# Reordered semaphore waits, a new table of places and 18 spare matmuls per chunk in a one-core AdaLN, Mamba and mixture-of-experts block

## What is computed

```
mod = silu(c) @ wmod                        # six rows of 256 per sequence: sa ca ga sb cb gb
h = layernorm(x) * (1 + ca) + sa
x = x + ga * mamba(h)                       # rmsnorm, in_proj, causal conv of 4 taps, silu,
                                            # x_proj -> dt, B, C; delta = softplus(dt_proj(dt))
                                            # scan over the sequence: s = s*exp(delta*A) + delta*B*u
                                            # y = sum_s(s*C) + u*D; out_proj(y * silu(z)) + h
h = layernorm(x) * (1 + cb) + sb
x = x + gb * (shared(h) + routed(h))        # 16 experts, top 4 by a sigmoid gate
```

## Time and profile before

| | before |
|---|---|
| median of 3 runs | 2980.88 us (2977.16 to 2983.09) |
| profiled execution, its time | 2980.19 us |
| profiled execution, its span | 2978.4 us |
| PE / DVE / ACT / POOL busy | 2431.5 / 2277.2 / 2129.4 / 2397.0 us |
| mean granted TensorE clock | 0.922 of 2.4 GHz |
| HBM read and written | 166.29 MB, 17.87 MB |

### The profile page before, as it was taken

The page is one execution under the profiler, slowest core; times in us unless marked ns, Lnnn a source line. Parts: engine busy times, 40 slices in busy tenths (PEclk is TensorE's granted clock), DMA queues, the critical chain, the costliest instruction groups (busy, mean ns, idle before and its releaser), DMA issues.

```text
span 2978.4 us, 52216 instructions
## 1 busy us (share of the span) xinstructions
PE 2431.5 (82%) x16084; PEld 1908.7 (64%) x16084; DVE 2277.2 (76%) x3495; ACT 2129.4 (71%) x4033; POOL 2397.0 (80%) x2382
## 2 busy tenths in 40 slices
PE   3557988888797888979888797888979788897879
PEld 1335767667576665757667575766757666676767
DVE  4777778787787878778787877878777787877753
ACT  4786877778686777868677787767868777785641
POOL 1887898889788888888888888888978878897842
PEclk7657999999899999999999899999989999998999
DMA  1775777867676785767677677776757777676841
GB/s 67 195 172 127 167 159 164 179 135 161 147 170 157 165 177 132 163 158 162 155 156 178 138 163 158 156 171 150 167 135 169 160 165 172 135 159 140 179 102 57
DMA packets 154563, 455.99 MB, mean 153 GB/s; under 512 B 22280, under 2 KB 24968, under 8 KB 154032
## 3 DMA queue, kind: packets, MB, share of 16 engines
q0 software_dynamic: 73728, 268.47, 48.2%
q1 hardware_dynamic: 80560, 184.20, 19.9%
HBM read 166.29 MB, written 17.87 MB: 62 GB/s over the span
## 4 chain that ended last, share of the span: by engine, by line
POOL 21%; issue 20%; PE 18%; DVE 15%; ACT 14%; DMA 6%; DVEq 1%; POOLq 0%; ACTq 0%; SPq 0%
POOL db_sb L669 10%; PE bank_ps L1413 8%; DVE states L1150 5%; PE moe_ps L1431 4%; POOL y_sb L681 3%; POOL act L712 3%; DMA y_sb<-c_rows 3%; DMA th_p<-x_dram 3%; ACT c_rows L886 3%; ACT da_ps L913 3%; PE rows_ps L1349 2%; DVE bank_ps L1097 2%; POOL y_sb L690 2%; DVE act L1231 2%; DVE act L1237 1%
## 5 line engine op out<-in xcount | busy, mean ns | idle before, releaser
L669 POOL TENSOR_TENSOR db_sb<-du_sb,b_sb 128x512 f32<-128x512 f32 x1024 | 1575.2, 1710 | 80.3 <-DVE states L1150 79.8
L886 ACT ACTIVATE c_rows<-rows_ps,xd_sb 128x512 f32<-128x512 f32 x1024 | 684.8, 684 | 186.4 <-PE rows_ps L1349 93.9
L1349 PE MATMUL rows_ps<-ident,states 128*128 128x128 f32 x4096 | 646.8, 291 | 177.6 <-ACT c_rows L886 104.9
L913 ACT ACTIVATE da_ps<-delta,a_sb 128x512 f32<-128x512 f32 x1024 | 704.4, 692 | 93.2 <-DVE states L1150 91.5
L712 POOL TENSOR_TENSOR act<-act,w_sb 128x256 f32<-128x256 f32 x512 | 580.8, 1185 | 224.7 <-DMA w_sb<-w_dram 119.4
L681 POOL DMA_DIRECT2D y_sb<-c_rows x512 | 608.2, 1195 | 149.9 <-DMA y_sb<-c_rows 77.1
L1431 PE MATMUL moe_ps<-eout_sb,act 128*128 128x256 f32 x2304 | 621.5, 395 | 103.8 <-POOL act L712 101.6
L1150 DVE TENSOR_TENSOR_SCAN states<-da_ps,carry,db_sb 128x512 f32<-128x512 f32 x512 | 649.3, 1276 | 54.1 <-ACT da_ps L913 52.3
L1349 PEld LDWEIGHTS rows_ps<-ident,states 128*128 128x128 f32 x4096 | 512.6, 150 | 273.8 <-DVE states L1150 123.6
L1413 PE MATMUL bank_ps<-h2T_high,ein_w_high 128*128 128x256 f16 x2304 | 643.2, 279 | 36.0 <-DVE h2T_low L1133 15.0
L1150 DVE TENSOR_TENSOR_SCAN states<-da_ps,db_sb 128x512 f32<-128x512 f32 x512 | 617.4, 1215 | 69.2 <-ACT da_ps L913 68.3
(11 more groups left out here) (169 smaller groups left out, 2633.8 us busy)
## 6 DMA issues: line engine op xcount, KB each, us to landing
y_sb<-c_rows POOLq DMA_DIRECT2D x512, 512.0 KB, 5.5
b_sb<-b_dram SPq DMA_DIRECT2D x128, 512.0 KB, 5.1
w_sb<-w_dram SPq DMA_DIRECT2D x256, 256.0 KB, 4.4
th_p<-x_dram SPq DMA_DIRECT2D x16, 512.0 KB, 8.2
r_dram<-conv SPq DMA_DIRECT2D x16, 512.0 KB, 2.8
x<-r_dram SPq DMA_DIRECT2D x16, 512.0 KB, 5.8
out_dram<-x SPq DMA_DIRECT2D x32, 256.0 KB, 2.3
mod_p<-mod_dram SPq DMA_DIRECT2D x7, 384.0 KB, 11.2
```

The lines of the kernel that those rows point to most:

```text
L669: pool.tensor_tensor(db_sb[:, n % NDB, :], du_sb[:, slots[t][0][0], b, :], b_sb[:, k % NBPAIR, s % BPAIR, :], ALU.mult).then_inc(sem["scal ...
L886: ac.activation(c_rows[:, n % NCR, j % CPAIR, :], rows_ps[j % 2][:, :], ACT.Copy, scale=xd_sb[:, slots[t][0][0], j, s:s + 1]).then_inc(sem ...
L913: ac.activation(da_ps[n % NDA][:, :], delta[:, slots[t][0][0], b, :], ACT.Exp, scale=a_sb[:, b, s:s + 1]).then_inc(sem["exp_done"], 1)
L1349: last = pe.transpose(rows_ps[j % 2][:, b * P:b * P + P], states[:, step % 2 * NB + b, j * P:j * P + P], ident[:, :])
```

## The change

There are four parts, with no change in what is computed.

1. In seven steps the waits are written in another order or cut down: `scaled` has `scan_done` first, `e_weigh` has the bank's semaphore first, `x_norm` has `x_rstd_done` first, `dtp` has the read of `xd` first, `rows` has `c_scales` first for j above 0, `tap` waits for `xi_centered` and then `halo_set` at k = 0 and for the tap before it alone at k above 0, and `dt_low` waits for both copies of `dt_high`.
2. The table of places is new throughout: `SHIFT`, `PLACE`, `FIRST`, `LAST`, `START` and the scalars. `PLACE` now has an entry for nearly every step.
3. `keep_awake` puts 10 matmuls of 128x256 f16 ahead of `y_t` of j = 0, and 8 ahead of `h2_t` of k = 0, into the bank that this step is about to fill.
4. `r_load` and `z_tanh` of the first mixed chunk wait for `ein_low_done`.

```diff
-SLOT = 70.6876
+SLOT = 70.5981
-SHIFT = {"b_load": -2.314, ... "c_add": 0.79, ... "w_t": 1.126, ... "y_gate": -0.101, ...}
+SHIFT = {"a_made": 2.299, ... "c_add": 1.155, ... "w_t": 1.841, ... "y_gate": -0.262, ...}
...
                     def scaled(t, s, b):
+                        if n >= NDB:
+                            pool.wait_ge(sem["scan_done"], n - NDB + 1)
                         pool.wait_ge(sem[f"b_in{k % NBPAIR}"], 16 * (k // NBPAIR + 1))
...
-                        pool.wait_ge(sem["scan_done"], max(0, n - NDB + 1))
...
                     def e_weigh(t, u):
+                        pool.wait_ge(*bank_read(("expert_in", t, u)))
                         pool.wait_ge(sem[f"w_in{k % NWROWS}"], 16 * (k // NWROWS + 1))
-                        pool.wait_ge(*bank_read(("expert_in", t, u)))
...
                     def x_norm(t, half):
+                        ac.wait_ge(sem["x_rstd_done"], nP(t) + 1)
                         ac.wait_ge(*bank_room(key))
-                        ac.wait_ge(sem["x_rstd_done"], nP(t) + 1)
...
                     def tap(t, b, k):
-                        v.wait_ge(sem["halo_set"], n + 1)
-                        v.wait_ge(sem["xi_centered"], n + 1)
-                        v.wait_ge(sem["tapped"], (CONV - 1) * n + k)
+                        if k:
+                            v.wait_ge(sem["tapped"], (CONV - 1) * n + k)
+                        else:
+                            v.wait_ge(sem["xi_centered"], n + 1)
+                            v.wait_ge(sem["halo_set"], n + 1)
...
                     def rows(t, s, j):
-                        pe.wait_ge(sem["scan_done"], (step + 1) * NB)
-
                         before = (step, j - 2) if j >= 2 else (step - 1, j + 2)
+                        if j == 0:
+                            pe.wait_ge(sem["scan_done"], (step + 1) * NB)
                         if before[0] >= 0:
                             pe.wait_ge(*c_scales(*before))
+                        if j > 0:
+                            pe.wait_ge(sem["scan_done"], (step + 1) * NB)
...
                     def y_t(t, j):
+                        if j == 0:
+                            keep_awake(("y_t", t, 0), 10)
...
+                    def keep_awake(key, n):
+
+                        pe.wait_ge(*bank_room(key))
+                        for _ in range(n):
+                            pe.matmul(bank(key)[:, 0:2 * P], in_w16[0][:, 0, 0:P], in_w16[0][:, 0, 0:2 * P], start=True, stop=True)
...
                     def h2_t(t, k):
+                        if k == 0:
+                            keep_awake(("h2_t", t, 0), 8)
```

More of the change, by code:

```diff
@@ L160 @@
-PLACE = {"b_load_0": 0.173, "b_load_3": -0.295, "b_load_4": 0.013, "b_load_7": 1.807, "c_scale_2": 0.046, "carry_0": -0.001,
[52 rows of a table removed]
-FIRST = {"b_store": 0.125, "dt_bias": 0.034, "dt_high": -0.092, "dtp": 0.026, "ein_low": -4.541, "h_rms": 0.889, "h_scale": 0.293,
-         "hn_high": -0.177, "hn_low": -1.03, "in_low": -1.842, "r_add": -0.475, "soft_ln": -0.603, "tap": 0.219, "u_tanh": 1.112,
-         "x_load": 0.132, "x_rstd": 5.921, "x_scale": -0.544, "xi": 2.127, "xi_copy": 0.024}
-LAST = {"e_mul": -0.008, "e_weigh": -0.199, "expert_in": -0.512, "expert_out": -0.749, "h2_high": 0.25, "h2_low": 0.658, "h2_t": 0.387,
-        "op_gate": -0.447, "out_add": 0.012, "r_load": -3.075, "w_load": 0.015, "w_store": -2.166, "w_t": -0.691, "x1_norm": -0.005,
-        "x1_rstd": -1.397, "x1_stat": 0.167, "y_evac": 0.514, "z": -0.362}
@@ L219 @@
-START = {"constants": 0.018, "ct_tanh": -1.588, "first_loads": 5.582, "fold": 1.987, "in_high": -3.563, "in_low": 0.718, "mod0": 0.251,
-         "mod_rows": -0.032, "mod_store": -0.045, "mods": 1.704, "out_scale": -2.535}
+LEAD_P0, LEAD_P, LEAD_M = 16.5692, 7.9826, 18.1414
+TICK, ROUTED, UNITS_END = 1.4598, 16.0092, 63.8809
+SOFT = 45.3931
+Z_AHEAD, Y_SOON, Y_LATE = 0.8485, -5.3218, 0.8267
+SLOT = 70.5981
+SHIFT = {"a_made": 2.299, "b_load": -0.655, "b_store": -0.03, "c_add": 1.155, "c_scale": 0.694, "carry": 0.739, "constants": 6.369,
+         "ct_silu": 7.993, "ct_tanh": 5.83, "delta": -0.292, "dt_bias": -0.13, "dt_high": -0.389, "dt_low": -0.659, "dtp": -0.013,
+         "du": 0.224, "e_act": -0.2, "e_mul": -0.161, "e_tanh": -0.423, "e_weigh": 0.864, "ein_high": 5.595, "ein_load": 4.207,
+         "ein_low": 1.18, "eout_fold": -4.167, "eout_load": 10.16, "exp": 1.021, "expert_in": -0.233, "expert_out": 0.79,
+         "first_loads": 0.924, "fold": 2.039, "gather": 0.59, "h2_high": 0.858, "h2_low": 1.341, "h2_scale": 0.171, "h2_t": 1.098,
+         "h_rms": -0.968, "h_scale": -0.068, "h_square": -0.404, "hn_high": -0.18, "hn_low": 0.343, "hn_t": -0.781, "in_high": -2.432,
+         "in_low": -2.541, "logit": -0.221, "logit_exp": 2.022, "mod0": 0.093, "mod0_gate": 9.566, "mod0_rows": 8.026,
+         "mod_m_load": -2.113, "mod_p_load": -4.442, "mod_rows": 8.536, "mod_store": -10.248, "mods": 6.814, "norm_lift": -8.849,
+         "op": 1.435, "op_gate": 1.25, "out_add": 0.237, "out_gate": 0.005, "out_scale": -12.936, "out_store": 1.491, "r_add": 3.969,
+         "r_gate": 0.223, "r_load": 1.079, "r_store": -6.015, "router": 1.458, "rows": 0.368, "scaled": 0.661, "scan": -0.15,
+         "skip": 0.192, "skip_evac": 0.341, "skip_t": 0.166, "soft_exp": -1.198, "soft_ln": 0.767, "tap": 0.086, "u": -0.826,
+         "u_tanh": 0.017, "w_evac": 0.533, "w_load": -0.824, "w_store": -2.476, "w_t": 1.841, "x1": 1.398, "x1_norm": -0.282,
+         "x1_rstd": -1.462, "x1_stat": 1.215, "x_load": -1.249, "x_norm": 0.894, "x_rstd": 0.076, "x_scale": 0.261, "x_shift": 0.165,
+         "x_stat": 0.314, "xd": -0.63, "xd_evac": -0.536, "xd_t": 0.416, "xd_t_evac": -0.528, "xi": 0.233, "xi_center": 0.049,
+         "xi_copy": 0.007, "y_evac": 0.755, "y_gate": -0.262, "y_t": 0.841, "z": -0.858, "z_gate": -0.839, "z_tanh": -0.616}
@@ new lines @@
+PLACE = {"b_load_0": 0.352, "b_load_1": 3.063, "b_load_2": 7.901, "b_load_3": -5.114, "b_load_4": 0.869, "b_load_5": 3.166,
[49 rows of a table added]
+         "in_low": 0.416, "logit": 0.537, "logit_exp": 0.204, "mod_m_load": -1.192, "mod_p_load": 0.549, "op_0": 0.553, "op_1": 0.135,
+         "op_2": 0.151, "op_3": -5.521, "op_gate_0": -0.207, "op_gate_1": -0.256, "op_gate_2": 0.574, "op_gate_3": -9.207,
+         "out_add_0": -0.142, "out_add_1": -0.151, "out_gate_0": 0.018, "out_gate_1": -0.445, "out_store_0": 1.142, "out_store_1": 2.785,
+         "r_add": -0.421, "r_gate": 0.252, "r_load": 0.166, "r_store": 4.589, "router": -0.089, "rows_0": -0.061, "rows_1": -0.193,
[21 rows of a table added]
@@ new lines @@
+FIRST = {"b_store": -1.691, "delta": -7.942, "dt_bias": -5.55, "dt_high": 0.322, "dt_low": 0.284, "dtp": -0.316, "du": 15.142,
+         "ein_high": 2.29, "ein_load": 1.427, "ein_low": -2.424, "h_rms": -7.043, "h_scale": -2.667, "h_square": 0.779, "hn_high": -2.392,
+         "hn_low": -2.331, "hn_t": -1.045, "in_high": 9.103, "in_low": -7.464, "r_add": -2.869, "r_gate": -3.859, "r_store": 9.187,
+         "skip": 0.46, "skip_evac": 7.151, "skip_t": 2.867, "soft_exp": 3.454, "soft_ln": 1.178, "tap": 0.991, "u": 2.33, "u_tanh": 0.596,
+         "x_load": -1.459, "x_norm": 0.639, "x_rstd": -0.049, "x_scale": 0.35, "x_shift": 0.09, "x_stat": 2.908, "xd": -5.521,
+         "xd_evac": -1.259, "xd_t": 0.226, "xd_t_evac": -0.902, "xi": -4.74, "xi_center": 1.94, "xi_copy": -0.671}
@@ new lines @@
+LAST = {"e_act": -0.086, "e_mul": 0.001, "e_tanh": 0.024, "e_weigh": 5.36, "expert_in": 0.948, "expert_out": 1.413, "h2_high": 1.147,
+        "h2_low": -2.551, "h2_scale": -1.666, "h2_t": -3.41, "logit": 1.396, "logit_exp": 0.191, "op": -0.871, "op_gate": 0.209,
+        "out_add": 1.16, "out_gate": 0.978, "out_store": -0.147, "r_load": 1.398, "router": 0.022, "w_evac": -1.369, "w_load": 2.655,
+        "w_store": 2.436, "w_t": 0.633, "x1": 0.207, "x1_norm": -3.031, "x1_rstd": -2.619, "x1_stat": 0.228, "y_evac": 0.006,
+        "y_gate": -0.421, "y_t": -0.772, "z": -3.279, "z_gate": -0.688, "z_tanh": -0.619}
@@ L223, in place @@
+START = {"a_made": 0.992, "constants": -1.608, "ct_silu": -9.647, "ct_tanh": -6.912, "first_loads": 4.989, "fold": 3.908,
+         "in_high": -10.598, "in_low": 4.148, "mod0": -2.429, "mod0_gate": 0.385, "mod0_rows": 0.709, "mod_rows": -3.599,
+         "mod_store": -7.158, "mods": -4.917, "norm_lift": 9.587, "out_scale": 0.531}
 def place(what):
@@ L571, in r_load @@
                     def r_load(t):
+                        if nM(t) == 0:
+                            sp.wait_ge(sem["ein_low_done"], NPAIR)
                         if nM(t):
```

6 lines of the change are left out of this document (4 added, 2 removed), and 122 rows, old and new, of the table PLACE.

## The result

The changed kernel takes 2877.03 us, the median of 4 runs (2876.35 to 2879.60), beside 2981.85 us for the kernel before (4 runs, 2977.16 to 2983.09). The ratio is 0.9653, 95% interval 0.9636 to 0.9670: 3.5% faster. I forecast 2943 us and a range of 2893 to 3005. The time lies 66 us under the forecast and 16 us under the range, in the case "more than I sum", to which I gave a chance of 0.10. The profiled execution has a span of 2874.6 us, 103.8 us less than before.

A forecast was written before the change was run, and what follows sets the result against it. No engine was taken as the bound: four almost equally busy engines share the chain. From 2980.2 us, waits -12, places -20, spare matmuls +3 and their clock -8 gave 2943 us, range 2893 to 3005.

The forecast's parts named there:

- more than I sum: Rival: POOL's holes and PE's waits close together, 27 and 62 us off, 2891 us (2870 to 2905); chance 0.10.
- What bounds the kernel: Whole kernel: no engine is the bound; a saved microsecond is worth between the engine's chain share (POOL 0.21) and one.
- Part 1, the waits: Reordered waits on POOL, PE and DVE: shorter hops save 27 us of engine time, taken as 12 us, at most 27.
- most taps stay neighbours: `tap` on DVE: most taps still follow one another in the new order, so shorter hops save 11 us, at most 16.6.
- Part 2, the places: New table of places: moved due times give a net gain of 20 us, bounds a gain of 95 and loss of 60.
- `e_weigh` u=2: POOL: due 3.9 us later, where it stood 4.51 us for weights; up to 62 us of idle time, taken as 20.
- `y_gate`: `y_gate` of j=0, 4.7 us later behind two more `scaled`: costs nothing, or 13.5 us if PE then waits for it.
- several hundred small moves that I can't price singly: The rest of the table of places: left unpriced, with no term of its own in the sum.
- Part 3, the spare matmuls: PE ahead of `y_t` and `h2_t`: 18 matmuls a slot cost 3 us and give back 8 us through a higher clock.
- Only the local parts count: Rival: the places trade one stall for another, POOL's weight wait becoming a scan wait; 2963 to 2987 us, chance 0.22.
- The `c_rows` buffers decide: Rival: `c_scale` on ACT waits for adds to free buffers, slack 4.0 to 2.4 us; slower, 2990 to 3060, chance 0.20.
- The signs that I named: Changed profile: no separate `e_weigh` wait, `w_sb` waits below 80 us, slot 173 us, clock above 0.9, ACT's add wait within 150.

The follow-up runs named there:

- w_only: The kernel before with the new order of waits, on the old table of places and without the spare matmuls: ratio 1.0011 to the kernel before, 2986 us.
- no_awake: The changed kernel without the 18 spare matmuls per chunk: ratio 0.9641 to the kernel before, 2875.5 us.
- weigh_old: no_awake with all `e_weigh` steps put back at their old due times: ratio 1.0031 to the kernel before.
- adds_old: no_awake with `scaled` and `c_add` alone put back at their old due times: ratio 0.9985 to the kernel before.

## Why the prediction was wrong

**What bounds the kernel: right, and read wrongly.** "A microsecond saved on one engine is worth a fraction of a microsecond" led me to multiply by POOL's chain share, 0.21. But the share is not a price: it went from 0.21 to 0.35 in w_only at no change in time. The `b_load` pair's hole, 36.9 us in 15 waits, gave 42 at the end, and 51.2 us cost 50 on the new table: a factor of one within the 7 us that can be told, not a fifth. `e_weigh` 2 gave 18 for 64. The factor has to be asked for each hole: what POOL does next, and whether that is ready.

**Part 1, the waits: hops right, worth wrong.** From `e_mul`'s end to a waiting `e_weigh` it is now 1354.49 - (1353.99 + 0.42) = 0.08 us, as forecast:

```profile
1353.99 0.42 DVE L1273 TENSOR_TENSOR act<-act,bank_ps 128x256 f32<-128x256 f32 x1
...
1354.49 0.72 POOL L744 TENSOR_TENSOR act<-act,w_sb 128x256 f32<-128x256 f32 x1 [1.80 <-DVE act L1273]
```

The separate wait instruction of `tap` is left 64 times out of 192, that of `e_weigh` still 512 times, but now it waits for the load, which has long landed:

```profile
L1131 DVEq EVENT_SEMAPHORE  x64: 21/21/730, 34.9 to 2502.2; - x64
```

```profile
L742 POOLq EVENT_SEMAPHORE  x512: 17/17/17, 283.0 to 2866.4; - x171
```

On PE, where `rows` waited for a `c_scale`, it starts 0.05 us after its end, the median of the 47 waits, for 0.14 before (0.05 forecast). Two taps in a row stand 0.04 us apart for 0.13. But only 40 of the 192 taps follow another tap directly in the old order and 70 in the new one, so "most taps stay neighbours" was wrong: the taps save 4 to 7 us and not 11. With the medians of the traces the shorter hops of `e_weigh`, `scaled`, `rows` and `tap` come to some 19 us on the old table, where I had 26 for them. They bring -12 us in my sum, and +3 on the old table, 4 to 9 us less on the new one. On the old table POOL's two waits before `e_weigh` are 228.3 us in w_only for 223.9 before, and its idle time 585 us for 581: there a shorter hop only lets the next wait begin sooner. The upper end of 27 that I let the hops have is out by the runs.

**Part 2, the places: the step that failed.** I put -20 us on it; it measures -98. Of the three moves that I named, `e_weigh` u=2 was sized right in the old table (20 forecast, 14 to 18 measured), and with luck: 62 us times a doubtful share happened to fit. I also read the 4.51 us of the earlier trace rows as a hole of every slot. The waits there are 60.1 us in 13, one of them the 22.0 us of the last mixed chunk. `y_gate` costs nothing, as forecast (PE's wait for it is 30.5 us for 29.8); the moves of `w_t` (5.5) and of `c_rows` (-5) were not run alone. What I left out is 42 us in one place: I compared POOL's, PE's and ACT's due times and never SP's. The row that would have told me was within what I read, the 119.4 us of waits for `w_sb` in 52 waits: the holes before `e_weigh` 2 leave 59 us in 39 others, 34.0 of them before `e_weigh` 22, and I didn't ask why weights whose buffer is free early come late. The other 54 us I had as "several hundred small moves that I can't price singly", at a value of nothing in the sum and without a reason for it; the 98 us measured lie at the edge of the gain of 95 that I gave as the bound.

**Part 3, the spare matmuls: clock right, worth nothing.** Counted from the clock's records over the 16 windows of 12 us around `h2_t`, PE was at half clock (1.2 GHz) for 108 of 192 us before, 68 without the spare matmuls in the new table, and 43 with them: the new order alone did more for the clock than the matmuls, which I had not foreseen. In one slot's windows around `y_t` and `h2_t`, of no_awake and then of the changed kernel:

```profile
913.80:921.80 8.00, 6.00 (x28) 4.35 (x29) 4.81 (x7) 5.15 (x11) 7.83 (x8) 0.79 0.47 121
931.20:943.20 12.00, 9.17 (x70) 7.86 (x71) 10.15 (x11) 11.74 (x24) 11.57 (x13) 0.72 0.71 176
```

```profile
913.90:921.90 8.00, 6.91 (x40) 4.52 (x39) 6.67 (x10) 6.43 (x17) 7.83 (x8) 1.00 0.56 146
933.10:945.10 12.00, 9.56 (x82) 7.72 (x82) 9.60 (x12) 11.71 (x23) 11.74 (x11) 0.86 0.84 197
```

The clock is higher here, 0.79 to 1.00 and 0.72 to 0.86 (in another slot both kernels have 1.00 and 0.86 already), and the end does not move. That POOL is busy in these windows for 7.83 of 8 and some 11.6 of 12 us, with PE idle for a quarter of them in no_awake, is the likely reason; no run tests it. My net of -5 us is nothing within what can be told. The Trainium skill, which I cited there ("TensorE: Matmul & The Clock Gate", under "What's actually happening"), puts the penalty of the ramp at under 1% of a typical kernel's span. This case does not speak against it: taking the spare matmuls out moved the ratio by 0.0012.

**The rivals.** "Only the local parts count" is refuted as a whole and shown in one place: POOL's wait for weights did turn into a wait for a scan, for 28 of 64 us. "The `c_rows` buffers decide" did not come: ACT's wait for the adds is 100.6 us in 51 waits, well under the 150 that I named. It shows in weigh_old (170.2 us in 95 waits), so the mechanism exists where the lists don't fit; in adds_old ACT's wait is 98.6. "More than I sum" is what came, by another way than I gave for it. I built it from the upper ends of parts 1 and 2, 27 and 62 us; neither was reached.

**The signs that I named.** Waits for `w_sb` under 80 us: 21.9. A slot of 173 us: 170.0. Clock above 0.9 around `y_t`: 1.00, but no_awake has 1.00 in one of two slots without the spare matmuls, and so has the kernel before (943 to 951 us), so this sign tells little. ACT's wait for the adds stays under 150 us and POOL's idle time falls. One did not come as I wrote it: `e_weigh` still has its separate wait instruction, 512 times, though the hop is 0.08 us. The signs looked at places that did move, but at none where the rest of the gain was.
